# GpSimd's place of waiting for gathered rows and for ring room in a graph aggregation

## What is computed

```python
xn = _layernorm(x, axis=-1)
msg = xn[edge_src]                                              # 100000 rows of 256
agg = jax.ops.segment_sum(msg, edge_dst, num_segments=n)
deg = jax.ops.segment_sum(jnp.ones_like(edge_dst, dtype=x.dtype), edge_dst, num_segments=n)
h_neigh = agg / jnp.maximum(deg, 1.0)[:, None]
out = relu(xn @ W_self + h_neigh @ W_neigh + b)
x = x + out + mix(xn)
```

## Time and profile before

| | us |
|---|---|
| median of 3 runs | 2771.84 |
| the 3 runs | 2755.1, 2781.39, 2771.84 |
| span of the profiled execution | 2754.8 |
| GpSimd's first gather starts | 110.0 |
| GpSimd's last gather starts | 1397.4 |
| TensorE's last matmul of the aggregation starts | 1423.2 |

### The profile page before, as it was taken

One profiled execution on the slowest core, in us unless ns is written; L12 is line 12 of the kernel. 1 busy time (PEld: TensorE's weight loads), 2 busy tenths in 40 slices (PEclk: granted clock), 3 DMA queues, 4 the chain that ended last, 5 costly groups with the idle time before them and its releaser, 6 DMA issues. The chain is left out here.

```text
span 2754.8 us, 27682 instructions
## 1 busy us (share of the span) xinstructions
PE 1979.1 (72%) x7431; PEld 1319.4 (48%) x7431; DVE 1364.5 (50%) x2602; ACT 888.2 (32%) x1940; POOL 1479.2 (54%) x1515
## 2 busy tenths in 40 slices
PE   5678778877766776676448688878878788884235
PEld 4444445445444454454327455556555555553223
DVE  6355433446655666565567433224424334246368
ACT  3423434443442434334315222222312223222124
POOL 2466555656656566556520666666656666661510
PEclk8789978988888888888765789999989999997555
DMA  5434222233433434335328512121211222215544
GB/s 182 136 126 130 83 77 77 84 103 115 138 98 117 135 109 137 107 101 181 92 85 262 189 35 49 35 69 35 69 35 43 61 47 58 50 36 169 157 142 153
DMA packets 197100, 283.01 MB, mean 103 GB/s; under 512 B 43074, under 2 KB 147491, under 8 KB 195810
## 3 DMA queue, kind: packets, MB, share of 16 engines
q0 software_dynamic: 61328, 115.27, 16.2%
q1 hardware_dynamic: 97218, 121.11, 13.3%
q10 hardware_dynamic: 38416, 44.96, 4.9%
HBM read 195.43 MB, written 85.81 MB: 102 GB/s over the span
## 5 line engine op out<-in xcount | busy, mean ns | idle before, releaser
L849 POOL DMA_INDIRECT ag_msg<-xn_tab,step_src x784 | 779.3, 994 | 509.7 <-PE ag_ps L1121 232.8
L1816 POOL DMA_INDIRECT edge_rows<-hx_d,gat_src x648 | 625.8, 966 | 349.0 <-issue 184.7
L1121 PE MATMUL ag_ps<-ag_msg,ag_hot 128*128 x1664 | 518.0, 454 | 189.7 <-DVE acc L871 97.5
L871 DVE TENSOR_TENSOR acc<-acc,ag_ps 128x257 f32 x832 | 351.7, 423 | 498.8 <-remote 190.3
L2004 PE MATMUL ex_psY<-co_rows 128*128 128x256 f32 x1568 | 421.3, 428 | 133.3 <-ACT co_rows L2058 73.2
L1121 PEld LDWEIGHTS ag_ps<-ag_msg,ag_hot 128*128 128x128 f32 x1664 | 339.9, 221 | 362.4 <-issue 316.4
L2004 PEld LDWEIGHTS ex_psY<-co_rows 128*128 128x128 f32 x1568 | 332.6, 216 | 219.1 <-ACT co_rows L2058 85.5
L1930 DVE TENSOR_TENSOR hi_one_low<-hi_numbers,hi_low 128x2048 bf16<-128x2048 f32 x64 | 146.4, 2287 | 500.1 <-remote 259.4
L1992 PE MATMUL ex_psF<-co_rows 128*128 128x448 f32 x896 | 351.5, 549 | 42.4 <-DMA ex_b<-in_b_dram 24.5
L1301 ACT ACTIVATE gat_self<-iota_row,step_nloc 128x128 f32<-128x128 f32 x832 | 258.5, 389 | 346.3 <-issue 202.6
L1992 PEld LDWEIGHTS ex_psF<-co_rows 128*128 128x128 f32 x896 | 170.8, 193 | 205.9 <-issue 158.9
(11 more groups left out here) (377 smaller groups left out, 2041.5 us busy)
## 6 DMA issues: line engine op xcount, KB each, us to landing
y_d<-co_rows ACTq DMA_DIRECT2D x28, 896.0 KB
co_rows<-y_d SPq DMA_DIRECT2D x28, 896.0 KB, 9.5
ag_msg<-xn_tab,step_src POOLq DMA_INDIRECT x784
xnT<-base_d SPq DMA_DIRECT2D x7, 1792.0 KB
edge_rows<-hx_d,gat_src POOLq DMA_INDIRECT x648
base_d<-xnT ACTq DMA_DIRECT2D x7, 1024.0 KB
sums_d<-edge_rows SPq DMA_DIRECT2D x5, 1344.0 KB
xg<-in_x_dram SPq DMA_DIRECT2D x7, 896.0 KB, 6.2
```

The source lines that it names most:

```text
L849: pool.indirect_dma_start(msg[:, q, u, 0:D], None, c.xn_tab, bass.IndirectOffsetOnAxis(ap=t.idx[:, at:at + 1], axis=0)).then_inc(s_g[q], 16)
L871: V.tensor_tensor(own, own, bank[u % BANKS][:, 0:ROWW], ALU.add).then_inc(s_acc, 1)
L1121: nc.tensor.matmul(bank[u % BANKS][:, 0:ROWW], hot[:, k, u, :], ring[:, ds(places[u - u0], ROWW)], start=True, stop=True).then_inc(s_mm, 1)
L1816: pool.indirect_dma_start(G[:, j % RING, w, :], None, c.hx_d, bass.IndirectOffsetOnAxis(ap=plan.idx[:, at + w:at + w + 1], axis=0)).then_i ...
```

## The change

Both waits are moved and come apart. After the eighth gather of half h GpSimd waits for the rows of that same half and adds 1 to `s_landed`. Ahead of the first gather of a half h from 4 on it loads the step number and waits for the room of half h itself (the last step that reads half h - 4). A semaphore `s_room` is added to, which nothing waits for. The order of all other engines stays as it was.

```diff
+        s_hot, s_mm, s_acc, s_init, s_landed, s_room = (c.sem("ag_" + n) for n in ("hot", "mm", "acc", "init", "landed", "room"))
...
                 for h in range(HALVES):
                     q = h % QUART
+                    if h >= QUART:
+
+                        at = h - QUART
+                        pool.wait_ge(s_mm, pool.value_load(t.freed[:, at:at + 1], min_val=2 * SBLK + 1, max_val=2 * SBLK + STEPS))
+                        pool.sem_inc(s_room, 1)
                     for u in range(SHALF):
-                        if h and u == SHALF // 2:
-                            if h + 1 in range(QUART, HALVES):
-
-                                at = h + 1 - QUART
-                                pool.wait_ge(s_mm, pool.value_load(t.freed[:, at:at + 1], min_val=2 * SBLK + 1, max_val=2 * SBLK + STEPS))
-                            landed(h - 1)
                         at = h * SHALF + u
                         pool.indirect_dma_start(msg[:, q, u, 0:D], None, c.xn_tab,
                                                 bass.IndirectOffsetOnAxis(ap=t.idx[:, at:at + 1], axis=0)).then_inc(s_g[q], 16)
-                landed(HALVES - 1)
+                    landed(h)
```

More of the change, by code:

```diff
@@ L699, in aggregate @@
         bank = [ps(f"ag_ps{i}", [P, 512]) for i in range(BANKS)]
-        s_hot, s_mm, s_acc, s_init, s_landed = (c.sem("ag_" + n) for n in ("hot", "mm", "acc", "init", "landed"))
+        s_hot, s_mm, s_acc, s_init, s_landed, s_room = (c.sem("ag_" + n) for n in ("hot", "mm", "acc", "init", "landed", "room"))
         ring = msg[:].rearrange("p q u r -> p (q u r)")
```

## The result

| | before | after |
|---|---|---|
| median us (4 runs each) | 2770.28 | 2801.09 |
| lowest and highest | 2755.1, 2781.39 | 2798.11, 2807.03 |
| span of the profiled execution | 2754.8 | 2804.7 |

The ratio on record is 1.0129, with a 95% interval of 1.0089 to 1.0169; at the medians it is 31 us slower, 1.0111.

What follows compares the result with a forecast made beforehand. Consumers were taken to set the pace before, GpSimd's chain after: 110.0 + 779.3 + 209.9 + 94 x 3.5 + 3 x 2.95 = 1437.0, stage some 20 us later; 17 on the median gives 2789 us, range 2764 to 2835.

Steps and rivals of the forecast that it cites:

- The stop: GpSimd at each half's end: landing, signal, number load and restart cost 3.5 us against 3.09 before; range 2.9 to 4.6.
- The number read bare: GpSimd's load of the step number, now behind the rows' wait: some 0.55 us exposed at 94 of 97 stops.
- Issuing: GpSimd's gathers: 779.3 us of issuing and 209.9 us of gaps within halves, taken over from the kernel before.
- The end: End of the aggregation: last issue ends at 1437.0, last signal 1439, TensorE wanted it at 1419.6; some 20 us later.
- TensorE's waits for the signal: TensorE at line 837, waiting for a landed half: to grow from 2.7 us to some tens.
- The consumers' own work covers GpSimd up to a stop of 3.3 us.: Aggregation: stops up to 3.3 us stay hidden; beyond that every 0.1 us costs 9.7 us over 97 stops.
- Hidden: Rival: a stop costs 3.3 us or less, GpSimd stays ahead, time unchanged at 2772 us; chance 0.23.
- The stretched landing: Rival: other queues' transfers lengthen landings; 2825 us if at a third of the stops, 2899 at all; chance 0.31.
- The faster one: Rival: bursts of gathers raise TensorE's clock in the aggregation, 0.90 instead of 0.84, 30 us less, 2742; chance 0.04.

Runs made afterwards that it cites:

- the repeat: The changed kernel itself, run again on a chip where the kernel before took 2757.72 us: 2795.72 us, ratio 1.0125.
- room asked of VectorE's count: Kernel before, with GpSimd's room wait on VectorE's count of finished adds instead of TensorE's of matmuls: 2288.96 us, ratio 0.9999, where the kernel before takes 2287.8.
- pauses: Kernel before, with six memsets of 128x512 on GpSimd after each half, waits in the middle: 2843.39 us, ratio 1.2418, where the kernel before takes 2287.8.
- the neighbouring version with half the stops: Kernel before, with both halves' rows awaited at every odd half, room wait in the middle: 2398.28 us, ratio 1.0472; on another chip 2739.16, ratio 0.9929.

## Why the prediction was right, and where it wasn't

The forecast was 2789 us, by GpSimd's chain; measured were 2801, inside the range, and the chain of GpSimd's issues and stops is the one forecast. Its picture of the kernel before was wrong, but with a stop of 3.56 us the chain binds either way, so that the number didn't hang on it. Between the two profiled executions 50 us came out, where 20 were forecast. That the medians lie only 31 apart is the spread of single executions, and so far the nearness of 2801 to 2789 is luck. Step by step:

- **The stop.** Forecast 3.5 us (landing 2.1, signal 0.05, number 0.55, restart 0.8), measured 3.557 with a landing of 2.14. 97 of them came to 345.0 us instead of 337.9. The Trainium skill, "DMA: Bandwidth & Descriptors", section "Anatomy of one DMA — SWDGE (gpsimd) path", gives 2.0 us plus the bytes at 436 GB/s, which makes, as an estimate, 1.35 us from the issue's end to the rows. Nine landings of ten took over 1.76, so here the rule was too short.
- **The number read bare, 0.55.** Right: reading it ahead of the landing took 0.46 off the mean stop.
- **Issuing, 989.2 us.** This is the term that was mis-sized: 1003.6. The gathers took 783.7 instead of 779.3 (776.8 in the repeat, so that this part is spread). The gaps within halves took 219.9 instead of 209.9, since seven of them are near 1.85 us rather than 0.3: behind gathers 113, 209 and so on to 689, one in 96. In the kernel before no gap outside the middles is over 0.5 us, and neither, but for the pauses, in the two kernels of its order on the quick chip (room asked of VectorE's count, pauses); the others have four to seven of them. So they came with the change, no row of before could have priced them, and why they come stays open.
- **The end.** Those two and a first gather 1.9 us later put the last issue's end at 1460.5 instead of 1437.0, and the last signal at 1463.6 instead of 1439. Against TensorE's need at 1419.6 that is 44 us instead of 20, and the last matmul moved by 45. The forecast was thus low by more than half in its own terms. On the median, 31 us came out against my 17. The profiled execution of before lay some 15 us under its median and that of after 6 above.
- **TensorE's waits for the signal**, forecast as "some tens": 333.3 us. Once GpSimd is the slowest, all the slack of its consumers turns into waits for it, also what they used to spend on each other (97.5 for VectorE became 12.8). I had priced only the excess.
- **"The consumers' own work covers GpSimd up to a stop of 3.3 us."** This step failed. With 3.09 and with 2.96 the time fell below that of before, by 0.6% and 1.1%. The prediction gave all 299.8 us of GpSimd's standing to TensorE's demand, though 61.1 of it had no named releaser. The consumers' pace in the kernel before was not their own work alone: VectorE's adds stood for 241 us behind counts that came late, and on a chip without late counts the consumers kept up with 10.6 us a half. On the chips of the result and of its repeat the change therefore did two things at once: it made GpSimd's chain longer, and most of the late counts went with it. How the 31 us net divide between them isn't settled.
- **Rivals.** Hidden fell by the stop's size. (The longest wait for room before was 12.78 us, not the 12.19 that the prediction read; nothing hangs on it.) The stretched landing exists (the tenth over 3.2 us), but not at a third of the stops. The faster one fell: the clock in the long stretch is 0.81, lower than before.

Open stays why a count comes late. What is shown is that it happens on one kind of chip and not on another with the same kernel. That it ends when GpSimd stops issuing is what single places in the trace suggest; the two runs meant to test it (pauses, and the other count) came to a chip where there was nothing to see, and halving the halts didn't scale it.

One rival is untested. The two kinds of chip also differ in what their traces hold. The 784 gathers add 16 each to their semaphores, 12544 updates in all. The trace of the kernel before has 3143 of them and that of the changed kernel 4876, but those of the quick chips have 12531 to 12544. Every execution on record has a span and a granted clock of its own, so it was recorded as it ran. Where records of counts go missing, the recording itself may be what holds the counts up, and with them part of the 2760 us. No run shows whether they come late without it.

## What to carry to other kernels

A wait for the youngest transfer costs its whole landing, and whatever the engine does before the next issue (here a number read for 0.55 us) is paid bare at every one of them; put it ahead of the wait. Of a change that moves two waits, run each half alone: here one half was neutral, the other a small gain on this kind of chip, and both together a loss. Before taking a wait for a sign of the consumer's work, look whether what it waited for was done long before: slack that comes from late counts isn't work, and it isn't there on every chip. Look, too, whether the trace holds all the updates that the program makes. And a few per cent found on one chip should be run on a second: rows awaited at the half's end gained 1.1% and 1.0% on two of them, and the neighbouring version with half the stops gained 0.7% on one and lost 4.7% on another.

## What the runs showed of the hardware

- The kernel before takes 2763 and 2758 us on two chips and 2288 and 2291 on two others. Of the 340 us between the two profiled executions of one version (rows awaited at odd halves) 127 lie ahead of the aggregation's last matmul (1408.9 against 1281.5) and the rest in the later stages. The adds and the issues take the same time on both. The profile's mark is "remote": on the quick chips no wait of any engine ends with it, in the kernel before on the other kind the counts for the experts, the copies of their rows and the adds have 259, 199 and 190 us of it. The granted clock of that version's two executions, 0.861 and 0.825, is nearer together than their times.
- In the kernel before, a semaphore count that TensorE had raised reached VectorE up to 11 us late, in places where GpSimd had been issuing gathers back to back. Of the count's updates on record, 146 stand under 0.1 us behind the one before, the closest 0.042, though the matmuls that raise it are at least 0.43 us apart; on the quick chips no two are closer than 0.43. Whether the recording has a part in it isn't shown.
- A gather of 128 KB lands 1.8 us behind the end of its issue in the median, and the mean is pushed to 2.1 to 2.3 by the tenth or so that takes over 3.2 us.
